# Product halves of 29 couples of groups, not 17, added ahead of the sums, in turn by GpSimd and by accumulating DMAs

## The reference

```python
e = jnp.stack([tbl_0[ids[:, 0]], ..., tbl_39[ids[:, 39]]], axis=1)
vi = x[:, i_idx, :]
vj = x[:, j_idx, :]
viW = jnp.einsum('bpd,pde->bpe', vi, W)
out = jnp.einsum('bpe,bpe->bp', viW, vj)
...
h = jnp.concatenate([z, dense_ctx], axis=1)
h = jnp.maximum(h @ W_top1 + b_top1, 0.0)
h = jnp.maximum(h @ W_top2 + b_top2, 0.0)
y = h @ W_top3
```

## Time and profile before

| | before |
|---|---|
| median of 3 runs | 349.3 us (348.85 to 350.2) |
| the profiled execution's own time | 349.04 us |
| its span in the profile | 346.9 us |
| PE busy | 329.1 us (95%) |
| DVE busy | 249.6 us (72%) |
| POOL busy | 225.6 us (65%) |
| POOL's gathers (line 265) | 144, 137.8 us busy, 41.9 us between them |
| POOL's adds (line 272) | 37, 86.8 us busy, 37.4 us idle before them |

### The profile page before, as it was taken

One profiled execution on the slowest core, in us unless ns is written; L12 is line 12 of the kernel. 1 busy time (PEld: TensorE's weight loads), 2 busy tenths in 40 slices (PEclk: granted clock), 3 DMA queues, 4 the chain that ended last, 5 costly groups with the idle time before them and its releaser, 6 DMA issues.

```text
span 346.9 us, 4306 instructions
## 1 busy us (share of the span) xinstructions
PE 329.1 (95%) x1676; PEld 115.1 (33%) x1676; DVE 249.6 (72%) x248; ACT 22.1 (6%) x35; POOL 225.6 (65%) x191
## 2 busy tenths in 40 slices
PE   0799979899999999999999999999999999999997
PEld 0133333233333333333333333333333333333442
DVE  2484968778787888978889888988888898840000
ACT  1001100000000000000001000010000000000032
POOL 6777777777778889877788788576887423520000
PEclk9999989999999999999999999999999999999999
DMA  6984443243423238731322323232110000000000
GB/s 167 255 231 146 119 106 105 81 102 91 115 57 104 64 96 261 170 104 33 96 85 62 89 68 86 62 69 85 39 23 2 0 3 0 0 2 0 0 2 0
DMA packets 17854, 27.59 MB, mean 80 GB/s; under 512 B 4901, under 2 KB 5029, under 8 KB 17834
## 3 DMA queue, kind: packets, MB, share of 16 engines
q1 hardware_dynamic: 9770, 17.86, 17.7%
q0 software_dynamic: 4608, 4.73, 6.9%
q10 hardware_dynamic: 3456, 4.72, 4.8%
HBM read 22.57 MB, written 0.00 MB: 65 GB/s over the span
## 4 chain that ended last, share of the span: by engine, by line
PE 80%; POOL 13%; issue 4%; DMA 1%; ACT 0%
PE ps_t L421 47%; PE ps_z L443 21%; POOL rows L265 13%; PE ps_t L465 5%; PE ps_e L404 2%; PE ps_t L488 2%; PE ps_e L465 2%; DMA rows<-in_tbl,ids_sb 1%; DMA ids_sb<-in_ids_t 1%; PE ps_t L494 1%; ACT y_sb L328 0%
## 5 line engine op out<-in xcount | busy, mean ns | idle before, releaser
L372 DVE TENSOR_TENSOR prod<-ps_t,E 128x1024 f32<-128x1024 f32 x200 | 231.7, 1217 | 45.7 <-PE ps_t L421 44.9
L421 PE MATMUL ps_t<-E,w_sb 64*128 64x512 f32 x800 | 189.8, 609 | 0.8 <-ACT E L294 0.7
L265 POOL DMA_INDIRECT rows<-in_tbl,ids_sb x144 | 137.8, 957 | 43.4 <-issue 41.9
L272 POOL TENSOR_TENSOR prod<-prod 128x1024 f32<-128x1024 f32 x37 | 86.8, 2370 | 37.4 <-DVE prod L372 37.3
L421 PEld LDWEIGHTS ps_t<-E,w_sb 64*128 64x128 f32 x800 | 71.1, 187 | 109.6 <-issue 82.2
L443 PE MATMUL ps_z<-prod,quads 128*32 128x512 f32 x572 | 76.8, 600 | 0.0
L443 PEld LDWEIGHTS ps_z<-prod,quads 128*32 128x32 f32 x572 | 15.1, 109 | 48.9 <-DVE prod L372 29.1
L351 DVE TENSOR_SCALAR prod<-prod,first_row_f 125x512 f32<-125x512 int32 x38 | 16.6, 495 | 11.1 <-PE ps_e L395 5.1
L294 ACT ACTIVATE E<-ps_e 128x512 f32<-128x512 f32 x18 | 10.8, 598 | 192.4 <-PE ps_e L404 171.1
L395 PE MATMUL ps_e<-prod 125*64 125x512 f32 x40 | 12.1, 694 | 11.2 <-DVE prod L351 10.0
L465 PE MATMUL ps_t<-z,w_sb 128*128 128x512 f32 (+1 forms) x42 | 18.6, 595 | 0.0
(11 more groups left out here) (26 smaller groups left out, 21.1 us busy)
## 6 DMA issues: line engine op xcount, KB each, us to landing
w_sb<-in_w_units SPq DMA_DIRECT2D x50, 256.0 KB, 2.9
E<-E ACTq DMA_DIRECT2D x72, 64.0 KB, 2.3
rows<-in_tbl,ids_sb POOLq DMA_INDIRECT x144, 2.6
w_sb<-in_w SPq DMA_DIRECT2D x7, 256.0 KB, 4.5
prod<-in_ids_by_field SPq DMA_DIRECT2D x2, 512.0 KB, 9.0
prod<-in_tbl SPq DMA_DIRECT2D x3, 312.5 KB
w_sb<-in_w SPq DMA_DIRECT2D x1, 512.0 KB, 7.1
prod<-in_tbl SPq DMA_DIRECT2D x1, 250.0 KB
```

Source lines behind the costliest of these rows:

```text
L265: pool.indirect_dma_start(rows[:, g % G_RING, b, f * DIM:(f + 1) * DIM], None, tables[2 * k + f], bass.IndirectOffsetOnAxis(ap=ids_sb[:, c ...
L272: pool.tensor_tensor(prod[:, n % P_RING, 0, :, :], prod[:, n % P_RING, 0, :, :], prod[:, n % P_RING, 1, :, :], ALU.add).then_inc(halves_ad ...
L372: dve.tensor_tensor(prod[:, n % P_RING, s, :, :], ps_t[:, (2 * n + s) % STEPS, :, :], multiplier, ALU.mult).then_inc(product_ready, 1)
L421: last = pe.matmul(ps_t[:, step % STEPS, j, :], w_sb[at:at + DIM, m % W_RING, col:col + P], E[at:at + DIM, slot_of(pairs_of(n)[s][j]), :], ...
```

## The change

`ADDED` becomes a table with one letter for each of the 50 couples: "P" for POOL's add as before, "D" for a DMA issued by POOL that accumulates s = 1 onto s = 0 in SBUF (512 KB read and 512 KB added to, for each group), "." for both halves summed by PE. There are 14 P (28 groups) and 15 D (30 groups): 29 couples. Against before, couples 8, 9, 10, 14, 16, 18, 20, 26, 28, 30, 32, 34, 36, 38, 42, 44 and 46 are new; couples 15, 23, 35, 39 and 47 are no longer added, nor are the three single groups. That is 17 new, 5 gone, 12 more.

```diff
-ADDED = [n for n, (_, M) in enumerate(GROUPS) if M is not None and n >= 20 and n // 2 % 2 == 1]
+ADDER = "........DPDP.PD.D.DPDP...DPPDPP.DPD.DPD..DPDPDP..."
+ADDED_BY_POOL = [n for n in range(NG) if ADDER[n // 2] == "P"]
+ADDED_BY_DMA = [n for n in range(NG) if ADDER[n // 2] == "D"]
+ADDED = sorted(ADDED_BY_POOL + ADDED_BY_DMA)
...
+        halves_added_by_dma = [sem(f"halves_added_by_dma{i}") for i in range(P_RING)]
...
             def add_halves(n):
                 pool.wait_ge(product_ready, 2 * n + 2)
+                if n in ADDED_BY_DMA:
+                    pool.dma_start(prod[:, n % P_RING, 0, :, :], prod[:, n % P_RING, 1, :, :],
+                                   accum_op=ALU.add).then_inc(halves_added_by_dma[n % P_RING], 16)
+                    return
                 pool.tensor_tensor(prod[:, n % P_RING, 0, :, :], prod[:, n % P_RING, 0, :, :],
                                    prod[:, n % P_RING, 1, :, :], ALU.add).then_inc(halves_added, 1)
...
                 for g in (n, n + 1):
                     pe.wait_ge(product_ready, 2 * g + 2)
-                    if g in ADDED:
-                        pe.wait_ge(halves_added, ADDED.index(g) + 1)
+                    if g in ADDED_BY_POOL:
+                        pe.wait_ge(halves_added, ADDED_BY_POOL.index(g) + 1)
+                    elif g in ADDED_BY_DMA:
+                        pe.wait_ge(halves_added_by_dma[g % P_RING],
+                                   16 * sum(a % P_RING == g % P_RING for a in ADDED_BY_DMA if a <= g))
```

## The result

| | before | changed |
|---|---|---|
| median | 349.53 us (4 runs) | 360.26 us (359.44 to 360.76, 4 runs) |
| ratio to before | | 1.0305, 95% interval 1.0276 to 1.0334 |
| span of the profiled execution | 346.9 us | 358.5 us |
| mean granted clock of PE | 0.995 | 0.976 |

The change costs 10.7 us where 6.3 was forecast: right in sign, inside the range (341.5 to 367) and its own range (351 to 362), and too small by 4.4 us.

The account below looks back on a forecast made before the run. PE was taken as the bound, with POOL's list the longest way from 94 to 247 us. Late additions of +8.9 us less 2.6 us of later short sums gave +6.3 us, 355.6 us; range 341.5 to 367.

Parts of the forecast that it names:

- its own range (351 to 362): Whole kernel: the range of the case slower as forecast, issue 0.9 to 1.4 us, landing 4 to 6; chance 0.48.
- Short sums, -10.3 us: PE's sums: four matmuls instead of eight save 0.86 us a couple, 12 couples net, 10.3 us in all.
- DVE's margin of 0: DVE's multiplications against PE with short sums: margin 0 us, at worst 0.1 us lost for each of 29 couples.
- Issue price d = 1.1: POOL's time to issue one accumulating DMA, taken as 1.1 us from the gather's row; ends 0.15 and 2.2.
- the rival of the cheap issue: POOL's issue costs only 0.15 to 0.5 us and landing 4 or less: 339 to 343.5 us; chance 0.24, DVE-bound included.
- POOL's walk: POOL's in-order list from 94 to 247 us against due times: late additions cost 8.9 us by couple 34's DMA.
- product 51: The walk's one crossing over DVE: product ready at 185.6 us, POOL waits for it and has issued its DMA at 186.7.
- Landing L = 5: Time from an accumulating DMA's issue on POOL to its landing, taken as 5 us everywhere; ends 2.3 and 9.0.
- a sign that POOL doesn't wait for DVE before 180 us: Sign that the forecast is right: POOL has no wait for DVE between 94 and 180 us.
- the forecast's own formula: Whole kernel's time change with issue price d and landing L left open: 17d + 2L - 22.4 us.
- The rival of the slow DMA (366): Accumulating DMAs pass data slowly or queue up, landing 9 us, issue 1.25: +17 us, 366 us; chance 0.20.

Follow-up runs that it names:

- Run 3: Changed kernel without the accumulating DMAs and PE's wait for them; all 29 couples' sums stay short, 15 leaving out half s = 1: 340.51 us.
- run 1: Changed kernel with the dense layers' weights loaded late, at the 19th pair of fields instead of the 12th: 356.78 us.
- run 8: Changed kernel with another table of 30 couples, 19 by POOL's add and 11 by DMA, and dense weights loaded late: 342.10 us.
- run 7: Changed kernel with all 29 couples added by accumulating DMAs, none by POOL's add, and dense weights loaded late: 365.26 us.
- run 6: Kernel before the change with one wait of PE added: couple 26's sum also waits for POOL's add of group 59: 357.26 us.
- run 4: Changed kernel with each DMA adding s = 0 onto unread s = 1, so DVE, not PE, waits for its landing: 353.15 us.
- run 5: Kernel before the change with one wait of PE added: couple 26's sum also waits for POOL's add of group 58: 352.66 us.

## Why the prediction was right, and where it was short

- **Short sums, -10.3 us:** right. Run 3 gives -9.2, and 0.89 of the rest is a wait for POOL's add at couple 9. DVE's margin of 0 held: 0.2 us at most for all 29 couples.
- **Issue price d = 1.1:** 0.97 measured, two in 1.95 us, and 0.30 of gap only when a gather follows. The nearest row, the gather, was the right guide; the rival of the cheap issue falls.
- **POOL's walk:** held. The adds of couple 9 were forecast to end at 111.2 and end at 111.86; three waits (9, 14, 16) stand where the walk put them, and couples 10 and 18 came late in run 1. It missed the wait at couple 30 (2.53 us), though its own times give one: from product 51's issue at 186.7 the list comes to the end of couple 30's adds at 227.7, and PE would come there at about 224.5.

```profile
107.19 4.67 POOL L281 TENSOR_TENSOR prod<-prod 128x1024 f32<-128x1024 f32 x2
111.79 1.94 POOL L278 DMA_DIRECT2D prod<-prod  x2
```

- **Landing L = 5:** this was the mis-sized term. The median from a DMA's own issue to its landing is 5.7 us, but the walk adds L behind both issues of a couple. Counted so, the landings that PE waited for in run 1 took 6.2 to 6.4 us at couples 10, 16 and 18; in the changed kernel they took 7.2 us at couple 14 and 10.3 at couple 16, which was forecast to land at 152.2 and landed at 157.5. The chain has it, counted from the first of the two issues:

```profile
145.28 0.60 POOL prod L278
145.88 11.67 DMA prod<-prod
```

  SP had queued the dense weights from 135.4 us on. L was one number for all places, though the trace before shows where the weights move (DMA share 0.85):

```profile
130.00:140.00 10.00, 10.00 (x58) 3.44 (x56) 8.40 (x8) 0.60 (x1) 9.38 (x6) 1.00 0.85 264
```

  Run 1 puts the weights' part at 4 us of landing and 3.5 us of the whole time. The Trainium skill (DMA: Bandwidth & Descriptors, "Issuing engines are not separate DMA queues") says that DMAs of all issuers interleave on the same 16 engines; the trace agrees, with a DMA share of 1.04 and 1.10 from 140 to 160 us. The Trainium skill's rule for a POOL-issued DMA (the same page, "Anatomy of one DMA"), 2.0 us plus bytes at 436 GB/s, gives an estimate of 3.2 us for this size, which is below the shortest landing here, 4.5 us.
- **The missing term:** slow clock after waits, 6.4 us. The forecast counted a wait at its length, and put nothing for the clock. Not all of it adds to the end: while PE ran slowly after couple 9, POOL caught up, and couple 10's wait of 3.45 us (run 1) was absent.
- **After the waits:** the forecast has the path on POOL's list from 94 us to the DMA of group 37 (159.3) and gives as a sign that POOL doesn't wait for DVE before 180 us. It does:

```profile
167.23 0.85 POOL L278 DMA_DIRECT2D prod<-prod  x1 [1.76 <-DVE prod L381]
170.79 4.68 POOL L281 TENSOR_TENSOR prod<-prod 128x1024 f32<-128x1024 f32 x2 [2.70 <-DVE prod L381]
```

  PE, held up at couple 16 and then slow, was the later of the two by then, and the chain runs from couple 16's landing over PE and DVE to product 51. That product was forecast for 185.6 and its DMA's issue began at 192.38, 6.8 late (0.8 of this is the start, 0.3 POOL's going on). From the end of that issue POOL's list took 40.9 us to the adds of couple 30, as worked out, but there the path passed to PE. At couple 34 PE waits 1.06 us for DVE, not for the accumulating DMA as forecast, and goes on at 256.98 where 251.75 was forecast: 5.2 late, or 4.4 without the start, the same 4.4 by which the median is off.

With d = 0.97 and L = 6.3 the forecast's own formula gives 17d+2L-22.4 = +6.7. So the lower d and the higher L nearly cancel, and the 6.3 came out close to that by this luck. What is left, 4 us, stands for the weights' 4 us at couple 16 and the 6.4 of slow clock together, which don't add in full; how they share it is not shown.

The rival of the slow DMA (366) names what happened at couple 16 of the changed kernel, but only there.

## What to carry to other kernels

Work that is taken off the bound engine and put into another engine's in-order list has to be priced by when it is done, against when the bound engine comes for it, not by that engine's total load: more load by 16 us (run 8) made it faster. Less load by 42 us (run 7) made it slower, but there the added DMAs also held each other up, so the engines that the work moves to need a price as well. Lay the list's times beside the due times, leave out the entries that come late, and count a long wait of a matmul engine at more than its length (4.8 us cost 7.7 in run 6).

## What the runs showed of the hardware

- An accumulating DMA of 512 KB between two places in SBUF: 0.91 to 0.97 us of POOL for each of several in a row, 4.5 us from issue to landing at best, 5.7 in the median, and 2.76 us of all 16 engines (an estimate from the queue's share). All 58 in one kernel took 9.8 us to landing in the median.
- From 88 us on, waits of PE of 1.95 us and more were in most cases followed by matmuls at close to half rate, which took 1.4 to 2.8 us more: waits of 2.53, 3.15 and 5.05 us in the changed kernel, 2.59 and 3.45 in run 1, 1.95, 3.05 and 3.15 in run 4, 4.76 in run 6, and 2.03, 2.15 and 7.04 in run 7. After 2.00 (changed kernel), 2.47 (run 5) and 3.06 us (run 1) they did not come, and after none of the waits of 1.83 us or less. It isn't the length alone: 3.06 us in run 1 left all lengths as they were, 3.05 us at the same sum in run 4 did not (16 product records in 5.40 us, not 3.70). What decides between the two stays open.
